# A six-layer decoder kernel on one core: no idle columns on TensorE, a sixth shared PSUM bank, and a first attention pass that runs four banks ahead

## What is computed

```python
x = x + _L0_attn_ref(_layernorm(x), L0_attn_w_qkv, L0_attn_w_proj)              # causal, 16 heads of 16
x = x + _L0_xattn_ref(_layernorm(x), ctx_768, mask_BxS2_bf1, ...)               # over 77 context rows
x = x + _L0_ffn_ref(_layernorm(x), L0_ffn_Wg, L0_ffn_bg, L0_ffn_We, L0_ffn_be)  # 8 linear experts, best 2
x = x + _L1_attn_ref(_layernorm(x), L1_attn_Wi, L1_attn_bi, L1_attn_Wh, L1_attn_bh)
x = x + _L1_xattn_ref(_layernorm(x), ctx_768, ...)
x = x + _L1_ffn_ref(_layernorm(x), ...)                                         # shared + 16 gated experts, best 4
```

## Time and profile before

| | us |
|---|---|
| median of three runs | 1408.14 |
| lowest and highest run | 1406.96, 1416.41 |
| span of the profiled execution | 1408.3 |

### The profile page before, as it was taken

How to read it: one execution, slowest core, us unless ns; L and a number is a source line. 1 busy time by engine, 2 the same in 40 slices (tenths; PEclk the granted TensorE clock), 3 DMA queues, 4 the chain that set the end, 5 groups by cost and what they waited for, 6 DMA issues and landing times.

```text
span 1408.3 us, 48623 instructions
## 1 busy us (share of the span) xinstructions
PE 1353.7 (96%) x19876; PEld 918.5 (65%) x19876; DVE 849.8 (60%) x2678; ACT 630.1 (45%) x2842; POOL 39.4 (3%) x60
## 2 busy tenths in 40 slices
PE   4798979999999999999999999999999999999998
PEld 2455436777756777776577777766667776765654
DVE  6757774268775225979661225758555565447585
ACT  2163304833524784253248876553253435433422
POOL 2000000000000000000000000000000000000000
PEclk9899989999999999999999999989999999989999
DMA  5746100021000002110000003310000200001000
GB/s 139 122 124 128 37 1 3 3 50 16 3 2 3 3 3 34 40 34 3 2 3 3 3 3 108 81 30 2 2 2 3 55 3 3 17 3 39 2 16 15
DMA packets 45471, 40.20 MB, mean 29 GB/s; under 512 B 9723, under 2 KB 44486, under 8 KB 45254
## 3 DMA queue, kind: packets, MB, share of 16 engines
q1 hardware_dynamic: 42662, 35.53, 11.1%
q10 hardware_dynamic: 2592, 1.57, 0.9%
HBM read 25.81 MB, written 10.80 MB: 26 GB/s over the span
## 4 chain that ended last, share of the span: by engine, by line
PE 90%; DVE 5%; DMA 1%; ACT 1%; issue 1%; SPq 0%; DVEq 0%; ACTq 0%
PE b L515 23%; PE b L1654 9%; PE b L534 8%; PE b L1431 6%; PE b L1023 6%; PE b L994 5%; PE b L1722 5%; PE b L939 4%; PE b L696 3%; DVE mx L948 3%; PE b L1300 3%; PE b L1275 2%; PE b L744 2%; PE b L459 2%; PE b L651 2%; PE b L501 1%
## 5 line engine op out<-in xcount | busy, mean ns | idle before, releaser
L515 PEld LDWEIGHTS b<-hp,whp 128*128 128x128 f16 x12276 | 472.1, 96 | 255.1 <-ACT hp L560 168.6
L515 PE MATMUL b<-hp,whp 128*128 128x2 f16 x12276 | 532.5, 165 | 1.0
L566 DVE TENSOR_TENSOR hp<-hist,hp 128x4 f16<-128x4 f32 x1023 | 164.5, 161 | 405.6 <-ACT hist L561 394.9
L560 ACT ACTIVATE hp<-b 128x4 f16<-128x4 f32 x1024 | 178.0, 174 | 442.8 <-PE b L515 430.2
L948 DVE TENSOR_REDUCE mx<-b 128x1 f32<-128x512 f32 (+3 forms) x304 | 189.9, 652 | 0.5 <-PE b L939 0.3
L1008 ACT ACTIVATE vp<-b 128x512 f32<-128x512 f32 x288 | 171.7, 603 | 17.7 <-PE b L997 9.8
L561 ACT ACTIVATE hist<-b 128x4 f32<-128x4 f32 x1024 | 177.2, 173 | 0.0
L534 PE MATMUL b<-whp 128*128 128x512 f16 (+6 forms) x608 | 162.1, 342 | 0.0
L1654 PE MATMUL b<-vp,heads 128*128 128x512 f16 x576 | 160.5, 380 | 0.0
L939 PE MATMUL b<-heads 128*128 128x512 f16 (+3 forms) x384 | 113.1, 333 | 5.8 <-DVE mx L948 2.8
L1431 PE MATMUL b<-we,xT 128*128 128x512 f16 x384 | 106.0, 383 | 0.0
(11 more groups left out here) (220 smaller groups left out, 1620.7 us busy)
## 6 DMA issues: line engine op xcount, KB each, us to landing
x_qs<-qx_scr SPq DMA_DIRECT2D x42, 128.0 KB
qx_scr<-xq_pair SPq DMA_DIRECT2D x16, 256.0 KB, 2.1
heads<-q_scr SPq DMA_DIRECT2D x24, 128.0 KB, 5.0
heads<-k_scr SPq DMA_DIRECT2D x36, 64.0 KB, 2.8
x<-in_x SPq DMA_DIRECT2D x8, 256.0 KB, 6.7
q_scr<-tail SPq DMA_DIRECT2D x8, 256.0 KB, 2.3
k_scr<-tail SPq DMA_DIRECT2D x8, 256.0 KB, 2.3
x_qs<-in_L_ffn_We SPq DMA_DIRECT2D x2, 1024.0 KB, 6.2
```

Of the source, the lines that this page charges most:

```text
L515: return pe.matmul(self.z(t)[:, m], self.w.whp[:, a, k, m * P:(m + 1) * P], self.g.hp16[:, (t - 1) % 2, part, k, :], start=False, stop=Tru ...
L560: act.activation(self.g.hp16[:, t % 2, 0], self.z(t), ACT.Tanh, scale=1 / LIFT).then_inc(self.s["hi_ready"], 1)
```

## The change

The item `idle` and all that plans it (`burst`, its constants) are taken out. The bank that it wrote, `g.b7`, joins the shared ones, which are six then. `FIRST_BANKS` is 4 instead of 3. Nothing else differs in the text; the planner makes a new order out of it. (The same diff, less blank lines.)

```diff
-FULL_CLOCK = 2300
-LEAST_GAP = 0.1
-BURST_STEPS = 1024
-BURST = 1.7
...
-        run = [0.0]
-        def burst(k):
-            if not k.chain or k.name != "hi" or k.next % BURST_STEPS != BURST_STEPS - 1:
-                return 0.0
-            return max(0.0, BURST - (free["pe"] - run[0]))
...
-                more = max((burst(k) for k in by_engine[e] if k.next < k.count), default=0.0)
...
-                        slack = max(late + max(0.0, at - k.ready - PATIENCE) * 0.1, more)
+                        slack = late + max(0.0, at - k.ready - PATIENCE) * 0.1
...
-                    key = (at, 0 if k.chain and not burst(k) else 1, k.rank(k.next))
+                    key = (at, 0 if k.chain else 1, k.rank(k.next))
...
-            if e == "pe":
-                gap = at - free[e] if last_chain and by_name["hi"].next else 0.0
-                if gap > LEAST_GAP or burst(k) > LEAST_GAP and by_name["hi"].next:
-                    if gap > LEAST_GAP:
-                        run[0] = free[e]
-                    more = burst(k) if gap <= LEAST_GAP else max(0.0, BURST - gap) * (burst(k) > 0)
-                    at += more
-                    self.order[e].append(("idle", int((max(gap, 0.0) + more) * FULL_CLOCK // 64) * 64))
-                elif gap > 0.05:
-                    run[0] = at
-                if k.chain:
-                    run[0] = at + cost
...
-FIRST_BANKS = 3
+FIRST_BANKS = 4
...
-        st.ops["pe"]["idle"] = self.idle
...
-    def idle(self, pe, columns):
-        for at in range(0, columns, 512):
-            pe.matmul(self.g.b7[:, 0:min(512, columns - at)], self.w.whp[:, 0, 0, 0:P],
-                      self.w.whp[:].rearrange("p a k n -> p (a k n)")[:, 0:min(512, columns - at)],
-                      start=True, stop=True, skip_group_check=True)
...
-        st = Stage(g, ctx, "", (g.b2, g.b3, g.b4, g.b5, g.b6), LATE)
+        st = Stage(g, ctx, "", (g.b2, g.b3, g.b4, g.b5, g.b6, g.b7), LATE)
```

## The result

The changed kernel takes 1484.49 us (median of four runs, 1466.52 to 1484.68) against 1409.46 us for the kernel before: a ratio of 1.0496 with a 95% interval of 1.0433 to 1.0560, so 5% slower. The direction was the one forecast (1430, slower); the size was not. The range ended at 1473, and the measured loss is 75 us where 22 were forecast.

The account below looks back on a forecast made before the run. Bounds taken: layer 0 work of the last chunk up to 997 us, the recurrence to 1273, then TensorE's gated experts. 1408.3 + 35 (falls) - 8 (idle columns' delay) - 5 (banks) = 1430.3 us; range 1392 to 1473.

Parts of the forecast that it names:

- The mechanism: Without idle columns TensorE is thin where they stood thickest, above all 300 to 450 and 550 to 750 us; clock falls.
- the falls (35 us): Clock falls where idle columns stood thick: 14 new ones at 2.5 us each, 35 us lost; ends 5 and 78 us.
- the banks (5 us): Sixth bank and four ahead in the first pass: TensorE runs ahead of VectorE, 5 us saved; bounds 0 and 19.2 us.
- The count of falls: One new fall in each of ten thick 50 us rows, a second in the four fullest: 14 new falls.
- The length of a fall: Each new fall lasts 13.6 us like both in the recurrence before; about 190 us more at 1.2 GHz.
- The price of a fall: Between nothing where TensorE has slack and 3.9 us where real matmuls follow each other; 2.5 us taken.
- The idle columns' own delay (8 us): Late idle columns gone: 3.6 us at half clock, 2 in the last stage, 2.4 elsewhere; 8 us saved, ends 5.6 and 22.
- Rivals 1 and 2: 1: the clock holds, 1395 us, chance 0.18. 2: falls come but cost next to nothing, 1402 us, chance 0.17.
- rival 3: The bank pays in full, 19.2 us in the first pass, with falls cheap: 1381 us, chance 0.07.
- Rival 4: Each of 14 falls costs half its length, as if TensorE's columns bounded every stretch: 95 us, 1490 us, chance 0.08.

Follow-up runs that it names:

- e1: The kernel before with only its idle columns taken out (five shared banks, three ahead, same order): 1513.92 us, ratio 1.0715.
- e5: The changed kernel with FIRST_BANKS back at 3 (six shared banks, no idle columns): 1489.23 us, ratio 1.0531.
- e2: The kernel before with FIRST_BANKS = 4 alone, idle columns and five shared banks kept: 1425.55 us, ratio 1.0108.
- e6: The changed kernel with three banks ahead and idle columns in planned gaps over 0.1 us, while a shared bank is free: 1432.29 us, ratio 1.0161.
- e12: The kernel before with four banks ahead and no idle columns, on five shared banks: 1536.66 us, ratio 1.0891.

## Why the prediction was right or wrong

**The mechanism held.** It was the clock, in the places named: the falls lie between 295 and 490, 575 and 793, 944 and 1030 us of the changed kernel and again from 1152 on, and taking out the idle columns alone gives more than the whole loss. What failed is the size of two terms: the falls (35 us) and the banks (5 us). For taking the columns out alone the prediction's terms make 35 - 8 = 27 us; e1 measured 101.

**The count of falls held.** 16 in the recurrence were forecast (14 new and the two of before); the trace has 18. Three pairs of these are only 3.4 us apart; taken as one each, they are 15.

**The length of a fall failed.** The prediction gave each the 13.6 us of the two in the kernel before, "about 190 us more". The 18 have 341 us together, 19 each, and the rest of the 406 us lies before the recurrence and at the end. Two cases of equal length, both from a kernel in which idle columns went on through the fall or dense work followed, were taken as a constant. Without the columns, in e1, a fall at 454.3 us ran on for 61 us and one at 952.6 for 78.5 us.

**The price of a fall was too small.** 2.5 us for 13.6 is 0.18 for each us at half clock. In e1, beside the same steps, it is 112.8 / 437 = 0.26; 0.30 to 0.35 in two stretches where TensorE sets the pace and about nothing where VectorE does. That a price lies between 0 and 3.9 us for 13.6 (0 to 0.29) was nearly right (single stretches of e1 go up to 0.39); "somewhat above the middle" was the wrong choice, because long falls reach into the dense second pass (28 of its exponentials stand in e1's stretch from 454.3 on). Both together: 406 - 65 = 341 us more instead of 190, at 0.26 and not 0.18, gives 89 us, where 35 stood in the sum. With what the order gains by the banks taken off (13 us, below), 76 is left of it, beside the measured 75. This is an estimate, and that it comes so near is in part luck: the price was measured in e1's recurrence alone, and the slope between executions (last section) would give some 20 us more.

**The idle columns' own delay (8 us) was too large or hidden.** Shortening each run by 0.08 us and adding 101 matmuls both left the time where it was, with intervals that reach 0.4% down and 0.2% up. The steps of e1 outside its half-clock stretches show it more directly: 715 steps without idle columns took 1.3 us less than the same steps with them, and 3.3 us less in the count most in the term's favour. So at full clock inside the recurrence the columns delayed next to nothing; the 2 us of the last stage stay open. That the shortened runs had some 20 us more at half clock and no longer time may mean a gain of a few us by less delay; this is only argued.

**The banks' term (5 us) was too small.** Sixth and fourth together are worth 1514 - 1484 = 30 us without idle columns. The step that failed is the sentence that in the dense stretches "I put no further term" for the other users of banks. It weighed the first pass alone, whose maxima indeed never waited, and that the fourth bank ahead gains nothing by itself was right (13 us lost on five banks with idle columns and 23 without; on six nothing that the runs resolve). The gain comes with the sixth bank, and it lies ahead of step 741. Windows of the first activation without idle columns, on five banks (e1), then on six (e5), both three ahead: the steps up to the wait for layer 0's last chunk, and this wait:

```profile
219.00:1049.00 830.00, 128.46 (x739) 0.80 0.09 18
1049.00:1089.20 40.20, 0.17 (x2) 0.84 0.01 2
```

```profile
223.00:1016.00 793.00, 128.24 (x741) 0.85 0.09 19
1016.00:1058.80 42.80, 0.31 (x2) 0.96 0.00 1
```

The first part went from 830 to 793 us. By the clock's record its time at half clock went from 338 to 232 us, which at 0.26 is an estimated 28 of these 37 us. So a good part of what the sixth bank gives comes by the clock. By the means of all executions e5 has 56 us less at half clock than e1 (401 against 457), 15 of the 25 us; the changed kernel has 391, so 17 of the 30 us, and 13 are left for the order. The wait itself is 37 us before and 26 in the changed kernel. Four ahead on five banks and six banks with three ahead (e2 and e6) have it thus (in e6 the window is 2 us longer than the wait):

```profile
970.00:1001.30 31.30, 0.17 (x2) 1.00 0.01 2
```

```profile
969.00:1012.00 43.00, 0.52 (x3) 1.00 0.01 1
```

So the fourth bank ahead shortens the wait, and the sixth does so only together with it; but in e2 the last stage loses more than the wait gains. Which of the banks' users gains by the sixth is open.

**The rivals.** Rivals 1 and 2 (the clock holds; the falls cost nothing) and rival 3 fell. Rival 4, 1490 us, came nearest in number but not by its mechanism: it had 14 falls at half of 13.6 us each. The rule of the Trainium skill on which that number also stood ("TensorE: Matmul & The Clock Gate", table of terms: time at the lower level times one minus the clock's share) would price 341 us at an estimated 170 us; measured beside the same steps was 0.26 and not 0.5, and only from 769.5 to 793.4 us does the step rate come near half of that beside it. The same page of the Trainium skill says in its section "A second HAM failure mode: psum-queue depth-cycling" that small pauses of TensorE between groups of matmuls make the clock swing, which fits the 18 falls here. No run separates such pauses from the few columns of the recurrence's matmuls, since the idle columns change both; half of the columns in the same gaps left about 210 us at half clock.

## What to carry to other kernels

Matmuls that compute nothing can be worth 7% of a kernel when TensorE waits often for another engine and dense work follows: ask of every one what the granted clock does without it, and try the edit alone. Price a fall of the clock by the work that stands behind the thin place, and beside the same steps of a kernel that differs in nothing else, not by the falls that the tuned kernel happens to have left. A bank can be worth more than its nearest user shows: the sixth gave 25 us here without idle columns. An edit that draws on it may cost without it: the fourth bank ahead lost 13 to 23 us on five banks and nothing on six.

## What the runs showed of the hardware that was not expected

Once down, the granted clock stayed at 1.2 GHz for as long as 78.5 us, through stretches in which TensorE's matmuls filled nearly all of the time: 58.63 of 61.40 us from 454.3 on in e1. Before the change its falls in the recurrence ended after 13.6 us.

Equal executions of one kernel differ by how much time they spend at half clock, and their times follow it: the changed kernel had 349 us and 1464.8 us of span in one execution and 406 us and 1483.0 in another, e1 430 and 1505.0, 497 and 1525.6, the kernel before 42 and 1401.2, 73 and 1411.5. That is 0.31 to 0.33 us for each us. A straight line through the executions of each of the thirteen changed kernels (this one and e1 to e12) gives 0.28 to 0.38, and the points lie close to it, so this is the greater part of the spread of their times. Why it is more than the 0.26 beside the same steps is open.
